# Expert stage of a Mamba-2 and mixture-of-experts layer: first weights by DMA per block, output bias in the last stage, 16 return buffers, mixed blocks in 64 columns

## The chip, the cores and the metric

The kernel runs on one core of a Trainium2 chip. The metric is the device time of one execution in microseconds. The engines are TensorE (PE, whose weight loads are shown as PEld), VectorE (DVE), ScalarE (ACT), GpSimd (POOL) and SyncE (SP), which issues most DMAs.

## The reference, cut to what matters

Input is 2048 rows of 128 values. A state-space layer with 16 heads is followed by a layer norm; its parts are not touched by the change. Then every row goes through 4 of 16 experts:

```python
logits = -dist2(x, keys) + x @ rw.T + rb            # 2048 x 16
topv, topi = top_k(logits, 4);  w = softmax(topv)
hidden = gelu(x @ w1[e].T + b1[e])                  # 128 -> 512
exp_out = hidden @ w2[e].T + b2[e]                  # 512 -> 128
fused = sum over the 4 chosen experts of w * exp_out
out = layernorm(x + fused)
```

All of it is float32. The tolerance leaves the kernel free to compute only the chosen experts.

## The kernel before, in words

The first 120 us compute the state-space layer for 16 tiles of 128 rows, in 8 pairs. For every finished tile the router finds the four experts, and POOL scatters the row, four times, with its expert numbers, row numbers and gates, to a table `xrows` in HBM that is sorted by expert (`send_one`, L1826). Two tables of blocks are built: one after five of eight pairs (`early_table`), for the first NE = 25 blocks, and one after all.

The expert stage then works on NBLK = 72 blocks of 128 rows. Blocks 0 to 63 (NF = 64) are full: all rows belong to one expert. Blocks 64 to 71 are mixed: the upper and the lower 64 rows belong to two experts. For a block b the work is

- SP reads the first row's place from the table `tbi` and issues the read of 128 rows into `xb` (`rows_in`, L446), in a ring of RB = 4
- PE turns the rows (`rows_transpose`, L741), ACT copies them from PSUM (`bt_copy`)
- DVE finds each row's gate and return address (`ids`, `row_ids`), copies the expert's first weights, their bias and the output bias, 644 columns, from the resident `w1s` into a ring (`take_w1`, L1372)
- PE multiplies by the first weights (`hidden`, L746), in four groups of 128 columns; ACT applies bias and GELU (`gelu`)
- PE multiplies by the second weights, which it reads in place from `w2s` (`expert_out`, L762)
- DVE adds the output bias (`out_bias`, L1385), ACT scales by the gate (`weigh`, L1745), POOL scatters the 128 rows to `yrows` in HBM (`give`, L1891), from one of four buffers `yw`.

Every engine runs its own list of steps, and in each step handles blocks at different lags; PE in step s turns the rows of block s+1, does the first layer of s and the second of s−1. Order inside an engine is written out by hand: steps up to 31 are single code (with parts of the router of the last two pairs of tiles between them on PE, DVE and POOL), then comes a loop of four steps per turn, then single code from step 60 on (`run_steps`, L107). Waits are on semaphores that count blocks.

The lines that the steps below touch:

```python
sp.dma_start(xb[b.slot(RB)][:], xrows[bass.ds(r, P), :]).then_inc(got[b.slot(RB)], 16)      # L465
ve.tensor_copy(w1c[r][:], w1s[:, bass.ds(expert_of(mybir.EngineType.DVE, b), 1), :]...)     # L1383
m = mm(hidden_bank(u)[:, f * P + h * HB:...], wh[:, f * P:(f + 1) * P], xbT[u][:, h * HB:(h + 1) * HB], ...)   # L755, mixed
```

Of the kernel before, what the change touches and what calls it, by code (L numbers as in the profile page):

```python
# [17 lines left out]
ALU = mybir.AluOpType  # L18
# [19 lines left out]
DE = D + 16  # L38
E, TOPK, F = 16, 4, 512
# [10 lines left out]
WB = F + FB + D  # L50
# [5 lines left out]
EPS_LN, EPS_RMS = 1e-5, 1e-6  # L56

class Step:
# [27 lines left out]

    def entry(self, h):

        return NF + 2 * (self.off - NF) + h  # L90

# [92 lines left out]
def block_and_moe(nc, d, debug=None):  # L184
    at, _ = const_table()
    with ExitStack() as ctx:
# [24 lines left out]
        w1s = sb("w1s", [D, E, WB])  # L211
# [3 lines left out]
        shared = sb("shared", [P, 8960])  # L215
# [21 lines left out]
        gmx = sb("gmx", [P, NP, 4 * HD * (CP + 1)])  # L237
        hx = sb("hx", [P, 4 * HD * (CP + 1) + CP * NP])
# [52 lines left out]
        xb = [view(ROW) for i in range(RB)]  # L291
        w1c01 = [view(WB) for i in range(2)]
        xbT = [view(P), view(P)]
        hT = [view(F), view(F)]
        sel8 = two("sel8", [P, 2, TOPK])
        idg = [sb(f"idg{i}", [P, 2]) for i in range(RB)]
        idi = [sb(f"idi{i}", [P, 1], I32) for i in range(RB)]
        yb = [view(D), view(D)]
        yw = [view(D) for i in range(RB)]
        w1c = w1c01 + [view(WB) for i in range(RB - 2)]  # L300
        w1d = [view(WB) for i in range(RB)]
        w2d = [view(FB, D) for i in range(2)]

        w1f, w2f = w1s[:].rearrange("p e f -> p (e f)"), w2s[:].rearrange("p e f d -> p (e f d)")
# [5 lines left out]
        y4 = [group_view(w1f, 0, g, TOPK * D) for g in range(NG)]  # L310
# [48 lines left out]
        def chunk_totals(g, k):  # L359
# [4 lines left out]
        ld = {k: sem("ld_" + k) for k in "cst small dtlow xT0 xT1 xT2 xT3 win wout won k idn w1 w2 b2".split()}  # L364
        zero_set, zero_out = sem("zero_set"), sem("zero_out")
# [5 lines left out]
        ksq_done, ksq_mm, kb_done, wo_done0, set_dve, ones_dve, bf_done, kw_dve, hs_set, gsum_dve, rw_dve, turn_set = (  # L371
            sem(n) for n in "ksq_done ksq_mm kb_done wo_done0 set_dve ones_dve bf_done kw_dve hs_set gsum_dve rw_dve turn_set".split())
# [6 lines left out]
        sent, sent2 = sems("sent", TOPK), sems("sent_late", TOPK)  # L379

        cnt_mm, c2, tb_mm, tab_done = (sem(n) for n in "cnt_mm c2 tb_mm tab_done".split())
        gm_set, c1, tb0_mm, var_dve, rv_pool, ge_pool = (sem(n) for n in "gm_set c1 tb0_mm var_dve rv_pool ge_pool".split())

        names3 = "bt_mm h_mm yb_mm bt_act w1_dve w2_act ht_act yb_dve yw_act c_id id_dve gt_dve"
        s3 = {n: sem(n) for n in names3.split()}
        got = sems("got", RB)
# [32 lines left out]
        def _(sp):  # L419
# [19 lines left out]

            sp.wait_ge(tab_done, 1)
            sp.wait_ge(s1["yi_mm"], NT - 2)
            for k in range(TOPK):
                sp.wait_ge(sent[k], 16 * 2 * EARLY)

# [1521 lines left out]
```

## Time and profile before

| | us |
|---|---|
| median of 3 runs (lowest, highest) | 383.8 (382.98, 385.81) |
| the profiled execution: span from first to last instruction | 313.4 |
| median less this span | 70.4 |
| PE, DVE, ACT, POOL busy | 273.5, 185.6, 214.7, 152.1 |
| mean granted clock of TensorE | 0.923 |

The profile lists the span of the profiled execution and not its own time outside it; the 70.4 us are taken from the median. The profile's page gives busy times, slices of the span, the chain of work that ended last and groups of instructions by line; the trace behind it is asked for windows, waits and single lines. "PE bank L760 x8" is eight halves issued by line 760. Register and DMA-issuing instructions of the queues are not counted as busy.

### The profile page before, as it was taken

To read this page: it belongs to the slowest core of one execution; us is meant where nothing else is said; L and a number is where in the kernel's file an instruction comes from. 1 tells how busy PE (TensorE), PEld (TensorE's weight loads), DVE (VectorE), ACT (ScalarE), POOL (GpSimd) and SP (SyncE) were. 2 spreads that over 40 slices of the span, in tenths; PEclk is the share of its full clock that TensorE was granted. 3 is DMA by queue.
4 is the path that set the end of the run, shared out by engine and by line. 5 is a ranking of instruction groups with operands and counts; after the bars stand their busy time and mean duration, and the time that the engine had idled before them with its cause. 6 is when DMAs were issued, how large, how long until landed. Compare 5 with 4: busy or idle time off the path is not lost.

```text
span 313.4 us, 11661 instructions
## 1 busy us (share of the span) xinstructions
PE 273.5 (87%) x3534; PEld 252.7 (81%) x3535; DVE 185.6 (59%) x817; ACT 214.7 (69%) x763; POOL 152.1 (49%) x167
## 2 busy tenths in 40 slices
PE   3989699988998757997996999999999999997591
PEld 3978577877787646997995999999999999995481
DVE  3135437877887865747876665566655566641272
ACT  1572538878787752784874688888888889884064
POOL 3103400037777677787677766555555564424000
PEclk9976679999999967799999799999999999999687
DMA  6999900001111212332232322222222222100973
GB/s 210 213 369 350 459 19 5 2 22 58 60 57 60 59 57 81 96 86 79 57 89 66 87 79 79 63 81 64 67 69 68 72 66 63 38 12 7 327 251 92
DMA packets 25408, 32.44 MB, mean 104 GB/s; under 512 B 4316, under 2 KB 18293, under 8 KB 25105
## 3 DMA queue, kind: packets, MB, share of 16 engines
q1 hardware_dynamic: 20576, 22.38, 24.2%
q0 software_dynamic: 4352, 8.79, 8.2%
q10 hardware_dynamic: 432, 0.67, 0.8%
q8 instruction: 26, 0.43, 0.6%
q14 instruction: 22, 0.17, 0.2%
HBM read 20.84 MB, written 11.50 MB: 103 GB/s over the span
## 4 chain that ended last, share of the span: by engine, by line
PE 74%; DVE 6%; ACT 6%; issue 6%; DMA 5%; SPq 1%; POOL 0%; ACTq 0%; POOLq 0%; DVEq 0%
PE bank L760 19%; PE bank L781 19%; PE bank L755 4%; PE bank L561 4%; PE bank L842 3%; PE bank L745 3%; ACT hs L1570 3%; PE bank L771 3%; PE bank L576 2%; PE bank L532 2%; PE bank L603 2%; PE bank L641 1%; DVE shared L962 1%; PE bank L548 1%; PE bank L845 1%
## 5 line engine op out<-in xcount | busy, mean ns | idle before, releaser
L1894 POOL DMA_INDIRECT yrows<-shared,idi x72 | 76.6, 1064 | 57.4 <-ACT shared L1752 33.3
L1826 POOL DMA_INDIRECT xrows<-rows_all,sli x64 | 62.1, 971 | 54.3 <-issue 50.7
L1733 ACT ACTIVATE shared<-bank,shared 128x128 f32<-128x128 f32 x256 | 72.9, 368 | 20.2 <-PE bank L760 19.8
L760 PE MATMUL bank<-shared 128*128 128x128 f32 x512 | 70.0, 281 | 6.0 <-issue 6.0
L760 PEld LDWEIGHTS bank<-shared 128*128 128x128 f32 x512 | 64.3, 197 | 7.3 <-issue 7.3
L781 PE MATMUL bank<-w2s,shared 128*128 x512 | 68.7, 278 | 0.1
L781 PEld LDWEIGHTS bank<-w2s,shared 128*128 128x128 f32 x512 | 63.1, 194 | 0.4 <-issue 0.3
L1383 DVE COPY shared<-w1s 128x644 f32 x64 | 33.0, 516 | 28.4 <-issue 27.3
L1752 ACT ACTIVATE shared<-shared,idg 128x128 f32<-128x128 f32 x72 | 30.0, 419 | 9.3 <-DVE shared L1396 7.9
L962 DVE TENSOR_TENSOR shared<-bank,small 128x512 f32<-128x512 f32 x32 | 21.2, 683 | 5.4 <-PE bank L576 5.2
L1719 ACT ACTIVATE shared<-bank 128x128 f32<-128x128 f32 x72 | 20.8, 289 | 4.5 <-PE bank L745 4.3
L745 PE MATMUL bank<-cst,shared 128*128 128x128 f32 x72 | 20.4, 283 | 2.0 <-DMA shared<-xrows 2.0
L561 PE MATMUL bank<-xT_all,winT 128*128 128x128 f32 x128 | 19.8, 304 | 2.0 <-issue 2.0
L561 PEld LDWEIGHTS bank<-xT_all,winT 128*128 128x128 f32 x128 | 17.6, 213 | 3.1 <-issue 3.1
L1396 DVE TENSOR_TENSOR shared<-bank,shared 128x128 f32<-128x128 f32 x64 | 18.4, 287 | 2.1 <-PE bank L781 0.5
L1364 DVE TENSOR_REDUCE idg<-sel 128x2 f32<-128x8 f32 x72 | 11.6, 161 | 11.6 <-ACT shared L1752 9.0
L1570 ACT ACTIVATE hs<-hx 32x128 f32<-32x128 f32 x32 | 13.8, 432 | 3.7 <-DVE hx L956 3.4
L1729 ACT ACTIVATE shared<-bank,shared 128x64 f32<-128x64 f32 x64 | 14.0, 330 | 2.5 <-PE bank L755 2.1
L755 PEld LDWEIGHTS bank<-shared 128*128 128x128 f32 x128 | 15.2, 194 | 0.2 <-issue 0.2
L755 PE MATMUL bank<-shared 128*128 128x64 f32 x128 | 15.3, 272 | 0.0
L1357 DVE SCALAR_TENSOR_TENSOR sel<-shared,tb 128x8 f32<-128x8 f32 x64 | 14.0, 218 | 1.9 <-issue 1.8
L576 PE MATMUL bank<-shared 32*64 32x128 f32 x512 | 12.8, 313 | 1.5 <-DVE hx L949 1.5
(233 smaller groups left out, 480.2 us busy)
## 6 DMA issues: line engine op xcount, KB each, us to landing
shared<-xrows SPq DMA_DIRECT2D x64, 70.0 KB
w1s<-in_w1T SPq DMA_DIRECT2D x1, 4128.0 KB, 23.0
w2s<-in_w2T SPq DMA_DIRECT2D x1, 4096.0 KB, 23.1
w1s<-yrows SPq DMA_DIRECT2D x8, 512.0 KB, 6.8
yrows<-shared,idi POOLq DMA_INDIRECT x72
xrows<-zrow SPq DMA_DIRECT2D x1, 1120.0 KB, 11.9
w1s<-in_b SPq DMA_DIRECT2D x1, 1024.0 KB, 22.4
xrows<-rows_all,sli POOLq DMA_INDIRECT x64, 2.4
```

Of the source, the lines that this page charges most:

```text
L561: m = mm(bank[2][:, k * P:(k + 1) * P], winT[:, c0:c0 + P], xT_all[:, t * P:(t + 1) * P], start=True, stop=True)
L745: pe.transpose(turned_rows(), xb[b.slot(RB)][:, 0:D], ident).then_inc(s3["bt_mm"], 1)
L755: m = mm(hidden_bank(u)[:, f * P + h * HB:f * P + (h + 1) * HB], wh[:, f * P:(f + 1) * P], xbT[u][:, h * HB:(h + 1) * HB], start=True, sto ...
L760: m = mm(hidden_bank(u)[:, f * P:(f + 1) * P], w[:, f * P:(f + 1) * P], xbT[u][:, :], start=True, stop=True)
L781: m = mm(out_bank(u), hT[u][:, f * P:(f + 1) * P], w2s[:, bass.ds(ex, 1), f, :], start=(f == 0), stop=(f == FB - 1))
L962: tt(sc[t % 4][:, r * HH:(r + 1) * HH, :].rearrange("p (b h) i -> p b h i", b=2), two_banks.rearrange("p b (h i) -> p b h i", h=H // 4), s ...
L1383: ve.tensor_copy(w1c[r][:], w1s[:, bass.ds(expert_of(mybir.EngineType.DVE, b), 1), :].rearrange("p o f -> p (o f)")).then_inc(s3["w1_dve"], 1)
L1570: m = act(hs[m_ % 2][rows, :, :, r * 2 * HD:(r + 1) * 2 * HD], chunk_states(m_)[rows, :, :, 0:CP].rearrange("p (j a) w c -> p c j (a w)", ...
L1733: m = act(hT[u][:, f * P:(f + 1) * P], hidden_bank(u)[:, f * P:(f + 1) * P], ACT.Gelu, bias=w[:, F + f:F + f + 1])
L1752: act(yw[r][:], yb[u][:], cp, scale=idg[r][:, 1:2]).then_inc(s3["yw_act"], 1)
L1826: po.indirect_dma_start(out=xrows, out_offset=bass.IndirectOffsetOnAxis(ap=sli[:, g, k:k + 1], axis=0), in_=rows_all[:, g, :], in_offset=N ...
L1894: po.indirect_dma_start(out=yrows, out_offset=bass.IndirectOffsetOnAxis(ap=idi[r][:, 0:1], axis=0), in_=yw[r][:, :], in_offset=None, bound ...
```

## The change

1. The first weights are no longer resident. SP issues, besides the row read, one DMA per full block from HBM (128 x 516 words, 258 KB) into a ring of four, and one for each of the 16 half blocks into 16 places that last until the end: seven in steps 25 to 31, eight in steps 56 to 63, one in step 64. PE waits for all 16 before the first mixed block.
2. The output bias leaves the blocks. DVE builds a 2048 x 16 table of gates in six operations in steps 25 to 30, PE turns it in step 31, and the last stage adds gates times b2 with eight products more. b2 lies in a block-diagonal buffer `b2d`, written by POOL's memset and eight small DMAs at the start.
3. DVE scales the block's output straight from PSUM (`weigh`); ACT's scaling and DVE's addition go.
4. The blocks before 30 return through 16 buffers, the later ones through 8.
5. In mixed blocks the first layer is cut into 64 output columns (16 products of 64 x 64 instead of 8 of 128 x 64), the rows are turned by two products, and the copy of the second expert's w2 moves from ACT to DVE.
6. POOL's root for the last tiles comes after six sends of tile pair 6 instead of eight; its eight last sends follow each other instead of alternating with returns. Some router functions on DVE change places. SP's loop is eight steps long, and the check of the table's value is left out.

```diff
-WB = F + FB + D
+WB = F + FB
...
+            def weights_in(b):
+                if b.had(RB):
+                    sp.wait_ge(s3["ht_act"], b.back(RB).count())
+                ex = expert_at(mybir.EngineType.SP, b.val())
+                sp.dma_start(w1c[b.slot(RB)], d["w1T"][:, bass.ds(ex, 1), :].rearrange("p o f -> p (o f)")
+                             ).then_inc(got_w[b.slot(RB)], 16)
...
+            def step3(s):
+                if s.live(NBLK):
+                    rows_in(s)
+                if s.back(1).live(NF):
+                    weights_in(s.back(1))
+                if s.peeled and NE <= s.off < LO3:
+                    mixed_weights_in(s.off - NE)
+                if s.peeled and NF - 8 <= s.off < NF:
+                    mixed_weights_in(LO3 - NE + s.off - NF + 8)
+                if s.peeled and s.off == NF:
+                    mixed_weights_in(2 * NM - 1)
...
-                pe.wait_ge(s3["w1_dve"], b.count())
...
+                    pe.wait_ge(ld["mixed"], 16 * 2 * NM)
                     for f in range(FB):
-                        for h, wh in enumerate((w, w1d[b.slot(RB)])):
-                            m = mm(hidden_bank(u)[:, f * P + h * HB:f * P + (h + 1) * HB], wh[:, f * P:(f + 1) * P],
-                                   xbT[u][:, h * HB:(h + 1) * HB], start=True, stop=True, skip_group_check=True)
+                        for h in range(2):
+                            for c_ in range(2):
+                                m = mm(hidden_bank(u)[c_ * HB:(c_ + 1) * HB, f * P + h * HB:f * P + (h + 1) * HB],
+                                       w1m[b.half(h)][:, f * P + c_ * HB:f * P + (c_ + 1) * HB],
+                                       xbT[u][:, h * HB:(h + 1) * HB], start=True, stop=True, skip_group_check=True)
...
+                pe.wait_ge(got_w[b.slot(RB)], b.weights_got(RB))
...
+            pe.wait_ge(gT_act, 1)
+            pe.wait_ge(ld["b2"], 16 * 8)
             for g in range(NG):
+                mm(to, gT[:, g // 4, :], b2d[:, k:k + GT * D].rearrange("p (t d) -> p t d", t=GT), start=False, stop=False)
...
+            def weigh(b):
+                ve.wait_ge(s3["yb_mm"], b.count())
+                if not b.early_ring() or b.last_put() > 0:
+                    ve.wait_ge(put[b.home()], b.last_put())
+                ts_(yw[b.home()][:], out_bank(b.slot(2)), idg[b.slot(RB)][:, 1:2], None, ALU.mult).then_inc(s3["yw_dve"], 1)
...
             def step3(s):
-                for fn, lag in ((ids, 0), (take_w1, -1), (row_ids, 2), (out_bias, 2)):
...
+                if s.back(-1).live(NBLK):
+                    ids(s.back(-1))
+                    row_ids(s.back(-1))
+                if s.back(1).live(NBLK):
+                    take_w2(s.back(1))
+                if s.back(2).live(NBLK):
+                    weigh(s.back(2))
```

On SP, one step of the loop was a table read, its check and address (ISA rows), and the row read (`shared` holds `xb`):

```order
L464 ISA
L464 TENSOR_LOAD tbi
L464 ISA x2
L465 ISA
L465 DMA shared<-xrows 128x140
```

Now the same step holds two table reads and two DMAs (`xbw` is the ring of rows, `w1r` the ring of first weights):

```order
L484 ISA
L484 TENSOR_LOAD tbi
L502 ISA
L502 DMA xbw<-xrows 128x140
L455 ISA
L455 TENSOR_LOAD tbi
L508 ISA
L508 DMA w1r<-in_w1T 128x516
```

The check of the value (`L464 ISA x2`) is gone, a table read and a DMA are added. In steps 25 to 31 and 56 to 63 a third pair follows, into the buffer `y4w` of the mixed blocks' weights:

```order
L484 TENSOR_LOAD tbi
L502 ISA
L502 DMA xbw<-xrows 128x140
L455 TENSOR_LOAD tbi
L508 ISA
L508 DMA w1r<-in_w1T 128x516
L455 TENSOR_LOAD tbi
L513 ISA
L513 DMA y4w<-in_w1T 128x516
```

On PE, a step of the mixed blocks began with the transposition of the next block's rows and the first layer in eight products:

```order
L745 MATMUL bank<-cst,shared 128x128
L755 MATMUL bank<-shared 128x64 x8
L412 TENSOR_LOAD tbi
L771 ISA
L771 MATMUL bank<-w2s,shared 64x128
L771 MATMUL bank<-shared 64x128
```

Now the rows are turned by two products, and the first layer has sixteen:

```order
L812 MATMUL bank<-cst,xbw 64x128 x2
L827 MATMUL bank<-shared,y4w 64x64 x16
L455 TENSOR_LOAD tbi
L845 ISA
L845 MATMUL bank<-w2s,shared 64x128
L845 MATMUL bank<-shared 64x128
```

The second layer (L771, now L845) is the same, and every product of the step now has 64 output columns. On DVE, a step of a full block was a copy of weights among five other operations:

```order
L1357 SCALAR_TENSOR_TENSOR sel<-shared,tb 128x8
L1364 TENSOR_REDUCE idg<-sel 128x2
L412 TENSOR_LOAD tbi
L1383 ISA
L1383 COPY shared<-w1s 128x644
L1371 TENSOR_TENSOR idi<-idg,pen 128x1
L1396 TENSOR_TENSOR shared<-bank,shared 128x128
```

Now four operations remain, and the last reads PSUM and the gate:

```order
L1445 SCALAR_TENSOR_TENSOR sel<-xbw,tb 128x8
L1451 TENSOR_REDUCE idg<-sel 128x2
L1458 TENSOR_TENSOR idi<-idg,pen 128x1
L1463 TENSOR_SCALAR shared<-bank,idg 128x128
```

The copy with its table read is gone, and gate and address of a block are computed one step before its rows are multiplied.

## Rows read from the trace of the kernel before

**Rows 1.** The page: PE's busy tenths and its granted clock in 40 slices.

```profile
PE   3989699988998757997996999999999999997591
PEclk9976679999999967799999799999999999999687
```

**Rows 2.** Five stretches: busy time of each engine, granted clock, DMA share, GB/s.

```profile
core 0: us, PE busy (x) PEld busy (x) DVE busy (x) ACT busy (x) POOL busy (x), PEclk, DMA share, GB/s
124.60:177.40 52.80, 46.62 (x401) 44.69 (x402) 36.61 (x191) 35.69 (x133) 39.32 (x40) 0.94 0.30 82
177.40:259.00 81.60, 81.60 (x734) 81.60 (x734) 49.17 (x217) 68.69 (x259) 46.41 (x44) 1.00 0.25 71
259.00:285.00 26.00, 24.93 (x273) 22.95 (x271) 14.34 (x55) 22.69 (x91) 10.23 (x10) 1.00 0.14 34
285.00:289.50 4.50, 3.69 (x16) 2.96 (x16) 0.51 (x2) 1.69 (x2) 2.65 (x3) 1.00 0.02 0
293.20:298.70 5.50, 5.50 (x13) 4.42 (x14) 1.89 (x7) 0.50 (x2) 0.00 (x0) 0.50 1.04 388
```

**Rows 3.** Chain of waits, two full steps and a mixed one: start, duration, what.

```profile
255.45 0.89 PE bank L760 x8
...
257.35 0.89 PE bank L760 x8
...
265.05 1.73 PE bank L755 x16
266.79 1.02 PE bank L771 x16
...
268.07 1.73 PE bank L755 x16
```

**Rows 4.** The page's groups: DVE's copy of weights; busy, mean ns, idle before.

```profile
L1383 DVE COPY shared<-w1s 128x644 f32 x64 | 33.0, 516 | 28.4 <-issue 27.3
```

**Rows 5.** Waits in 125 to 178 us: total, times, longest.

```profile
PEld bank L760 <- issue: 7.3, 6, 2.9
DVE rw L1023 <- POOL rv L1900: 3.2, 1, 3.2
```

**Rows 6.** Chain of waits on SP: the second row read from its table read on.

```profile
121.90 0.38 SPq L464
...
122.31 0.16 SPq L464
...
122.59 0.04 SPq L465
...
122.74 1.89 DMA shared<-xrows
```

**Rows 7.** DMA instructions on SP by line: ns least, median, most.

```profile
L465 SPq DMA_DIRECT2D shared<-xrows x64: 332/333/358, 121.5 to 249.5; - x64
L461 SPq DMA_DIRECT2D shared<-xrows x16: 477/477/566, 251.4 to 271.1; - x16
L474 SPq DMA_DIRECT2D w1s<-yrows x8: 400/472/583, 289.5 to 293.2; - x8
```

**Rows 8.** SP's own waits in 190 to 250 us: total, times, longest.

```profile
SPq L457 <- DVE idg L1364: 17.3, 31, 0.8
```

**Rows 9.** Chain: 64 x 64 products; page: GELU of mixed blocks.

```profile
52.90 0.69 PE bank L603 x16
...
L1729 ACT ACTIVATE shared<-bank,shared 128x64 f32<-128x64 f32 x64 | 14.0, 330 | 2.5 <-PE bank L755 2.1
```

**Rows 10.** Chain of waits at the end; output DMAs on SP.

```profile
283.79 1.11 PE bank L771 x16
...
287.28 2.11 DMA yrows<-shared,idi
...
289.47 3.69 DMA w1s<-yrows
...
L479 SPq DMA_DIRECT2D out<-w2s x16: 596/606/709, 300.8 to 310.9; - x16
```

More of the change, by code:

```diff
@@ L56, with early_puts @@
 EPS_LN, EPS_RMS = 1e-5, 1e-6
+def early_puts(home):
+    return len([b for b in range(EARLY_HOMES) if b % RE == home])
 class Step:
@@ L473, in _ @@
+            sp.wait_ge(tab_done, 1)
+            for k in range(TOPK):
+                sp.wait_ge(sent[k], 16 * 2 * EARLY)
+            run_steps(sp, step3, NF - 1, RY, LO3, NBLK)
+            for j in range(RE):
+                late_puts = len([b for b in range(EARLY_HOMES, NBLK) if b % RY == j])
+                sp.wait_ge(put[j], 16 * (early_puts(j) + late_puts))
             for g in range(NG):
@@ L778, in expert_out @@
                 if b.had(2):
[L779 removed]
+                    pe.wait_ge(s3["yw_dve"], b.back(2).count())
                 for f in range(FB):
@@ L1385, in out_bias @@
-            def out_bias(b):
-                u = b.slot(2)
-                ve.wait_ge(s3["yb_mm"], b.count())
-                if b.had(2):
-                    ve.wait_ge(s3["yw_act"], b.back(2).count())
-                if b.mixed():
-                    for h, wh in enumerate((w1c[b.slot(RB)], w1d[b.slot(RB)])):
-                        r = slice(h * HB, (h + 1) * HB)
-                        m = tt(yb[u][r, :], out_bank(u)[r, :], wh[r, F + FB:WB], ALU.add)
-                    m.then_inc(s3["yb_dve"], 1)
-                    return
-                tt(yb[u][:], out_bank(u), w1c[b.slot(RB)][:, F + FB:WB], ALU.add).then_inc(s3["yb_dve"], 1)
@@ new lines, in take_w2, with gate_rows @@
+            def take_w2(b):
+                if not b.mixed():
+                    return
+                if b.off >= NF + 2:
+                    ve.wait_ge(s3["yb_mm"], b.back(2).count())
+                ex = expert_at(mybir.EngineType.DVE, b.entry(1))
+                ve.tensor_copy(w2d[b.slot(2)][:].rearrange("p f d -> p (f d)"),
+                               w2s[:, bass.ds(ex, 1), :, :].rearrange("p o f d -> p (o f d)")).then_inc(s3["w2_dve"], 1)
+            def gate_rows(k):
+                h, what = divmod(k, 3)
+                t = slice(h * NT // 2, (h + 1) * NT // 2)
+                if k == 0:
+                    ve.wait_ge(s1["pk_act"], NP - 2)
+                if k > 0:
+                    ve.wait_ge(g_dve, k)
+                if what == 0:
+                    m = tt(gq, c("eids").rearrange("p (k e) -> p k e", k=TOPK).unsqueeze(1).broadcast_to([P, NT // 2, TOPK, E]),
+                           rows_all[:, t, RA:RI].unsqueeze(3).broadcast_to([P, NT // 2, TOPK, E]), ALU.is_equal)
+                if what == 1:
+                    m = tt(gq, gq, rows_all[:, t, RG:ROW].unsqueeze(3).broadcast_to([P, NT // 2, TOPK, E]), ALU.mult)
+                if what == 2:
+                    m = ve.tensor_reduce(gd16[:, h * P:(h + 1) * P].rearrange("p (t e) -> p t e", e=E),
+                                         gq.rearrange("p t k e -> p t e k"), AX_X, ALU.add)
+                m.then_inc(g_dve, 1)
```

317 lines of the change are left out of this document (166 added, 151 removed).

## The prediction

> **What bounds the kernel now.** I read the slices and the busy shares first: TensorE (PE) is busy in nine tenths of nearly every slice from the third on, and its granted clock is full except near 30, 125 and 295 us [rows 1]. Then a table by stretch [rows 2]. It cuts the expert stage in three. In 124.6 to 177.4 us, steps 0 to 20, PE is busy for 46.6 of 52.8 us. In 177.4 to 259.0, steps 21 to 63, it is busy for all 81.6 us. In 259.0 to 285.0 come the eight mixed blocks. After that PE works 3.7 us, stops, and runs at half clock until 298.7.
>
> The chain of waits shows what one step is. A full block repeats after 1.90 us (255.45 to 257.35; its first layer is eight halves in 0.89 us), a mixed one after 3.02 us, of which the first layer takes 1.73 and the second 1.02 [rows 3]. So in the middle 43 steps nothing but PE sets the time, and work taken off DVE or ACT gives nothing there. It can give something in steps 0 to 20, and the change can lose something anywhere if a new wait lasts longer than 1.90 us per block.
>
> **The change part by part.** One execution is worked through: its span is 313.4 us; the median of the runs is 383.8, so 70.4 us lie around the span and I leave them alone. Differences are made against the span.
>
> *First weights by DMA, steps 0 to 20.* DVE loses one copy per block: 0.516 us busy and, before it, 27.3/60 = 0.46 us for the register load of the expert's number [rows 4]. ACT loses the scaling of outputs. 21 steps at 1.90 are 39.8 us, the other PE work there (two groups of position counts, a transposition, an output product, the table) about 2.7, so 10.3 us of the 52.8 are surplus: PE waiting, and running at half clock (mean 0.94). What ended PE's waits at L760 is "issue", 7.3 us in 6 waits of the weight load, longest 2.9: these are waits for DVE's copy, which sat behind other DVE work, once behind the 3.2 us in which DVE waited for POOL's root of the last variance [rows 5]. POOL now computes that root two sends earlier. With about 0.9 us of DVE taken out of each step, DVE has room for the routing work between blocks. The 16 homes let POOL send its eight late rows in one go without holding DVE. I take half of the surplus as gone, 5.5 us; bounds 2 and 9. A new cost stands at the start: the first weights can be asked for only after two row reads. From 120.44 the two items and half a third end near 123.05, the transfer lands 2.4 us later (below) at 125.45, and block 0's first layer began at 125.00: +0.5. Net −5.0.
>
> *What SP has to issue, steps 21 to 64.* This is the part that speaks against the change. One row read on SP, from the table read at 121.90 to the landing transfer's issue at 122.74, is 0.84 us, plus 0.33 for the DMA instruction and 0.05 [rows 6, 7]. The usual table read is 0.27, not 0.38, and the address check (122.31 to 122.59, 0.28 us) goes. One item of the new kind is therefore 0.11 less and 0.28 less: 1.22 − 0.39 = 0.83 us. The wait for rows adds 0.05. A straight-written step is two items, 1.71 us; in the loop register arithmetic adds some 0.09 per item, and the branch 0.05 per block, so 1.96 us. Steps 25 to 31 and 56 to 63 carry a third item (a mixed block's weights): 2.55 us. Before, SP had room: in 60 us it waited 17.3 us over 31 blocks for DVE, 0.56 us a block [rows 8]. That room, plus the check, is 0.84; the added item is 0.83 and its registers 0.09. So SP is now longer than PE's 1.90.
>
> How much may SP lag? The ring of four weights is free for block b when the GELU of b−4 ends: the first layer ends 1.0 us into step b−4, ACT's whole work of a step is 68.69/43 = 1.60 us, nearly all of it GELU, so some 2.5 us into that step; 0.45 to the issue, then the transfer. Its landing I take as 1.89 us, the row read's [rows 6], plus the additional 188 KB at 388 GB/s [rows 2], 0.5: 2.4 (bounds 1.9 and the 3.7 of a 512 KB return [rows 10]). Needed at 7.7 us: slack 2.3. From the start of step 21, SP's third item of step 25 ends at 2.3 us, the next six steps at 17.6, 24 loop steps at 64.6, eight steps of three items at 85.0, step 64 (two half row reads at 0.83 + 0.14, since 64 partitions cost 0.477 against 0.333 [rows 7], and two weight items) at 88.7, the rows of block 65 at 90.7. They land 1.4 us later, so step 64 cannot start before 92.3. PE alone would need 81.5. So +10.8 us.
>
> The unknown is the instruction that issues 128 x 516 words from HBM: no row shows it. The nearest is the row read through a register, also 128 partitions, 0.333 us; returns are at 0.472 [rows 7]. I take 0.333 because form and register match. At 0.472 and some queue pressure (up to 0.583) 55 items cost up to 10 us more; at 0.30, a loop without branch cost, and a quicker landing, 4 us less, and if SP's overhead overlaps in a way I don't see, the whole 10.8 goes.
>
> What a page says here: the Trainium skill, DMA: Bandwidth & Descriptors, section Rules for kernel authors, says that spreading DMAs over several issuing engines doesn't help bandwidth and only saves the sequencer's issue time. By that rule issue time is a price of its own and one engine has to pay all of it; the trace agrees, with a landing of 1.9 us but the same 0.33 us instruction on each read. A reader who thinks of bandwidth alone (258 KB at 388 GB/s is 0.68 us of each 1.90, on top of a DMA share of 0.25) would put this part at nothing.
>
> *Mixed blocks.* Before, 16 halves with 128 weight columns and 64 moving ones take 1.73 us. After, 32 halves of 64 x 64. The same shape stands at L603: 16 halves in 0.69 us, the wait for the first result included [rows 9]. Bounds are 2 x 0.69 = 1.38 and 0.9 (twice what remains of 0.69 without about 0.24 of filling); I take 1.1. Two turned row halves replace a transposition, about equal. So a mixed step is 1.1 + 1.02 + 0.2 = 2.3 against 3.02. ACT has 14.0/8 = 1.75 us of GELU per mixed block [rows 9] and a copy of 0.29: under 2.3. DVE gets the copy of w2, but it ends about when PE wants it. SP's two half reads take 2.0. Six steps gain 0.72, step 64 0.7, the last one 0.85: −5.9.
>
> The Trainium skill, TensorEngine Tiling (Array Packing), section Restrictions, says column tiling disables the fast weight load. If 64-column loads were as long as L755's, 32 x 0.108 = 3.5 us, the mixed blocks would be 1.7 us slower each. L603 contradicts it: its 16 in 0.69 us are 0.043 each.
>
> *The end.* From the last expert product to the first read of returned rows are now 4.6 us: 284.9 to 289.47 [rows 10], with two steps on DVE, one on ACT and POOL still sending the block before. One DVE product from PSUM, 0.3, then the send and its landing 2.1, POOL free: 3.1. −1.5. The waits for 16 homes instead of 4 add up to 0.4, contained.
>
> *Last stage.* PE gets eight products of 256 columns, as long as the eight it has: 3.7 us [rows 2]. They lie before the first y4 data and beside its transfer, in a hole of 3.7 us. I also expect a gain: after that hole PE ran 5.5 us at half clock [rows 2], and the first output left late, after which SP issues sixteen outputs at 0.61 [rows 10] without a break. A filled hole keeps the clock at 2.4 GHz; half of 5.5 us comes back, less 0.6 for the last added product: −2.2. If the clock falls anyway, the added products cost up to +3.
>
> Sum: −5.0 + 10.8 − 5.9 − 1.5 − 2.2 = −3.8. Span 309.6, time 380.0 us. The earlier parts (5 MB less at the start, a longer POOL memset, six DVE products of 512 columns, two more transpositions) lie in gaps or under SP's queue and count zero; without that cover they cost 1 to 3 us.
>
> **Rivals.**
> 1. *SP keeps up.* If an item is 0.75 instead of 0.83, loop steps are 1.80 and only the three-item steps lag, mostly inside the slack of 2.3. For it: SP's instructions are short and the row queue waited 0.56 us a block. Against: the sum above is from single rows. Time 380.0 − 10.8 + 2 = 371.2.
> 2. *SP's weight issue is dear: slower.* Each of 39 block weights and 16 mixed ones takes 0.52 us (between 0.472 and 0.583) instead of 0.333. It decides from about 0.40 us, where the whole gain is used up. PE then waits over 2.1 us a step from step 21. 380.0 + 55 x 0.19 = 390.4.
> 3. *The early stage doesn't speed up*, because POOL's sends (0.97 us each, one after another) or DVE's order still set it: +5, 385.
> 4. *The change does nothing for mixed blocks*, weight loads being in line: +6 to +14 (the page's rule), 386 to 394. L603 speaks against it.
>
> **How the numbers follow.** Forecast 0.48, rival 1 0.18, rival 2 0.16, rival 3 0.14, rival 4 0.04. The forecast's own spread is 375 to 386, from item lengths of 0.80 to 0.87 over 95 items and the bounds of the early gain. A measurement of this kernel can tell about 1%, 3.8 us, from no change. Faster than 380.0: half of the forecast (0.24), all of rival 1 and a little of 3: 0.46. Slower than 387.6: rivals 2 and 4 and a little of the forecast: 0.20. The rest 0.34. The range takes in rival 1 and most of rival 2: 369 to 391.
>
> **What would show it.** PE's steps in the middle should grow from 1.90 to about 1.96 in the loop and 2.55 in steps 25 to 31 and 56 to 63, with PE waiting for w1 transfers, and SP's queue should stop waiting for DVE. Mixed steps at 2.3; the step before the first of them long. Steps 0 to 20 in 47 to 48 us. Granted clock full between 293 and 299. Wrong, if middle steps stay at 1.90 (rival 1), if SP's DMA for w1 is above 0.40 (rival 2), or if PE's surplus early stays at 10 us (rival 3).

## The result, and the profile after

The changed kernel takes 395.5 us (median of 4 runs, 394.88 to 398.84), the kernel before 383.39 (4 runs, 382.23 to 385.81): a ratio of 1.032, 95% interval 1.028 to 1.037. It is slower, and the time lies above my range of 369 to 391. Some kernels ran in two states a per cent or two apart, and the ratios here and below compare only executions in the faster one, so that they can differ a little from the quotient of the medians.

The profiled execution of the changed kernel took 395.21 us, and its span is 393.4. Only 1.8 us lie around the span. That alone overturns a sentence of the prediction, "70.4 us lie around the span": had it been so before, it would be so now. The page of the changed kernel:

```profile
span 393.4 us, 11573 instructions
PE 300.7 (76%) x3704; PEld 268.9 (68%) x3705; DVE 164.7 (42%) x742; ACT 190.3 (48%) x684; POOL 146.3 (37%) x168
PE   4987997594948583446499419998999987889893
PEclk9956899577786868585789857999999998999998
L834 PE MATMUL bank<-shared,w1r 128*128 128x128 f32 x512 | 73.7, 290 | 7.2 <-DMA w1r<-in_w1T 6.7
```

In rows 1, PE was busy in nine tenths of nearly every slice. Here it is not from the seventh slice (about 60 us) to the twenty-fourth, and the granted clock goes up and down. What runs there first is the scan of the state-space layer, which the change does not touch; the row sends begin in that slice (66.1 us). The last line is the first expert layer (L760 before): it waits 6.7 us for weights from HBM, the new wait that I had forecast.

I timed the middle and the mixed steps by when PE begins to turn the rows of a block (L816, and L812 for mixed ones). So "step 21" below is the start of that piece for block 21, and "steps 21 to 64" is the time from there to the same piece of block 64. (In the prediction a step begins when the rows of the block after it are turned, so its steps lie one block later.)

### The profile page after: what moved, and what is told of

The parts are those of the page before. It is cut to its first block, busy times and chain, and to the rows that moved or that the text cites. A ratio compares the mean times of both kernels' runs of the same rounds, so it can differ in the third digit from the quotient of the medians.

```text
span 393.4 us, 11573 instructions
## 1 busy us (share of the span) xinstructions
PE 300.7 (76%) x3704; PEld 268.9 (68%) x3705; DVE 164.7 (42%) x742; ACT 190.3 (48%) x684; POOL 146.3 (37%) x168
## 4 chain that ended last, share of the span: by engine, by line
PE 54%; issue 19%; SPq 11%; DMA 5%; ACT 4%; DVE 3%; another core or an unknown queue 2%; ACTq 0%; DVEq 0%; POOLq 0%; POOL 0%
PE bank L834 9%; PE bank L855 9%; PE bank L626 5%; PE bank L641 5%; SPq L455 3%; SPq L508 2%; PE bank L845 2%; PE bank L687 2%; SPq L502 2%; SPq L484 2%; PE bank L827 2%; PE bank L613 2%; ACT hs L1666 2%; DMA y4w<-yrows 2%
## 5 line engine op out<-in xcount | busy, mean ns | idle before, releaser
L1979 POOL DMA_INDIRECT yrows<-shared,idi x72 | 70.5, 979 | 83.2 <-DVE idi L1458 39.2
L1829 ACT ACTIVATE shared<-bank,w1r 128x128 f32<-128x128 f32 x256 | 72.9, 368 | 57.4 <-PE bank L834 34.7
L834 PE MATMUL bank<-shared,w1r 128*128 128x128 f32 x512 | 73.7, 290 | 7.2 <-DMA w1r<-in_w1T 6.7
L834 PEld LDWEIGHTS bank<-shared,w1r 128*128 128x128 f32 x512 | 66.9, 204 | 9.9 <-issue 8.1
L1463 DVE TENSOR_SCALAR shared<-bank,idg 128x128 f32<-128x128 f32 x72 | 25.2, 350 | 74.1 <-remote 24.6
L1815 ACT ACTIVATE shared<-bank 128x128 f32<-128x128 f32 x72 | 20.9, 291 | 29.6 <-remote 15.1
L816 PE MATMUL bank<-cst,xbw 128*128 128x128 f32 x64 | 18.7, 292 | 14.7 <-ACT shared L1815 7.7
L641 PEld LDWEIGHTS bank<-shared 32*64 32x64 f32 x512 | 12.9, 169 | 19.4 <-issue 18.6
L1050 DVE TENSOR_TENSOR shared<-bank,small 128x512 f32<-128x512 f32 x32 | 21.2, 683 | 10.1 <-PE bank L641 10.1
L626 PEld LDWEIGHTS bank<-xT_all,winT 128*128 128x128 f32 x128 | 21.5, 253 | 2.8 <-issue 2.6
L816 PEld LDWEIGHTS bank<-cst,xbw 128*128 128x128 f32 x64 | 9.4, 147 | 16.3 <-issue 16.2
L1445 DVE SCALAR_TENSOR_TENSOR sel<-xbw,tb 128x8 f32<-128x8 f32 x64 | 14.2, 221 | 13.2 <-DMA xbw<-xrows 10.5
L687 PE MATMUL bank<-shared,xz 128*16 128x64 f32 x512 | 13.8, 235 | 6.5 <-issue 3.8
L687 PEld LDWEIGHTS bank<-shared,xz 128*16 128x16 f32 x512 | 9.6, 104 | 8.6 <-issue 8.5
L1825 ACT ACTIVATE shared<-bank,y4w 128x64 f32<-128x64 f32 x64 | 14.0, 329 | 2.4 <-PE bank L827 2.1
```

The lines of the kernel that those rows point to most:

```text
L626: m = mm(bank[2][:, k * P:(k + 1) * P], winT[:, c0:c0 + P], xT_all[:, t * P:(t + 1) * P], start=True, stop=True)
L641: m = mm(bank[b][q * Q:(q + 1) * Q, j * P:(j + 1) * P], c_[rows, 2 + j, q * Q:(q + 1) * Q], cbd[t % 2][rows, j, q, :], start=True, stop=Tr ...
L687: m = mm(turned_y[32 * c_:32 * c_ + NC * HD, a * Q:(a + 1) * Q], xz[t % 4][:, h * NC * HD:(h + 1) * NC * HD], sc[t % 4][:, a % 2 * 8 + a / ...
L816: pe.transpose(turned_rows(), xb[b.slot(RB)][:, 0:D], ident).then_inc(s3["bt_mm"], 1)
L834: m = mm(hidden_bank(u)[:, f * P:(f + 1) * P], w[:, f * P:(f + 1) * P], xbT[u][:, :], start=True, stop=True)
L1050: tt(sc[t % 4][:, r * HH:(r + 1) * HH, :].rearrange("p (b h) i -> p b h i", b=2), two_banks.rearrange("p b (h i) -> p b h i", h=H // 4), s ...
```

## The experiments

**Is the base right? The two kernels once more.** No edit.

> The kernel before, unchanged, profiled and timed again. Theory A: every timed execution near 383 us has a span near 381 us, in which the scan stage runs slowly from the first row send (66 us) on, with pairs about 21 us apart as in the profile of the changed kernel; the span of 313.4 that I predicted from is of another, rarer kind of execution. Then the two kernels have to be compared with the slow scan in both, and the change costs 12 us against about 381. Theory B: the span is 313 in every execution and 70 us lie outside it; then the changed kernel's slow scan (pairs 21 us apart, 1.8 us outside the span) is something that the change brought in.

> The changed kernel, unchanged. Theory A: one more execution near 395 with pairs 21 us apart; there is a chance of one near 322 (395 less the 70 us), with pairs 10.6 us apart, as the kernel before showed once. Theory B: always 395.

Measured: before again 382.59 us (10 runs), its profiled span 384.0, beside 385.83 for that execution. The changed kernel 396.05, ratio 1.030 (1.021 to 1.040). Theory A holds. By stretch, the kernel before on this chip (scan from the fourth pair to step 0, early steps, middle, mixed, end; then the eight row sends of one pair, and the rest of that pair):

```profile
64.20:169.50 105.30, 67.17 (x1217) 53.63 (x1217) 44.05 (x189) 41.52 (x151) 41.52 (x43) 0.74 0.10 32
169.50:245.50 76.00, 52.15 (x388) 50.18 (x387) 37.52 (x196) 34.88 (x130) 40.08 (x40) 0.78 0.19 56
245.50:328.90 83.40, 82.14 (x734) 81.73 (x732) 48.57 (x216) 68.75 (x259) 47.78 (x44) 1.00 0.24 69
67.40:77.70 10.30, 5.82 (x92) 3.51 (x90) 0.70 (x2) 2.01 (x9) 7.90 (x8) 0.71 0.15 50
77.70:88.80 11.10, 9.53 (x162) 8.14 (x159) 7.56 (x30) 6.24 (x22) 0.00 (x0) 0.81 0.03 9
```

The columns are those of rows 2: length, then busy time and instructions of PE, PEld, DVE, ACT and POOL, the clock, the DMA share and GB/s. The same stretches in the profile that I predicted from:

```profile
63.50:123.60 60.10, 50.32 (x1217) 43.18 (x1217) 44.84 (x194) 41.96 (x151) 41.85 (x44) 0.91 0.17 56
66.70:76.80 10.10, 9.18 (x248) 7.97 (x247) 7.97 (x32) 8.17 (x29) 7.88 (x8) 1.00 0.16 54
```

The 1217 matmuls of the scan take 105.3 us here and 60.1 there. While eight row sends go, PE gets through 92 matmuls instead of 248. The weight loads of two neighbouring lines of the program show it, in the kernel before on this chip (start, length; in brackets the idle time before):

```profile
71.61 0.18 PEld L681 LDWEIGHTS bank<-oh,ones 128*128 128x128 bf16 x4 [0.51 <-issue]
71.81 0.18 PEld L576 LDWEIGHTS bank<-shared 32*64 32x64 f32 x1
72.35 0.30 PEld L576 LDWEIGHTS bank<-shared 32*64 32x64 f32 x3 [0.36 <-issue]
73.07 0.30 PEld L576 LDWEIGHTS bank<-shared 32*64 32x64 f32 x5 [0.42 <-issue]
74.52 0.34 PEld L576 LDWEIGHTS bank<-shared 32*64 32x64 f32 x5 [1.14 <-issue]
75.97 0.30 PEld L576 LDWEIGHTS bank<-shared 32*64 32x64 f32 x4 [1.10 <-issue]
```

Three to five pieces, a pause of 0.4 to 1.1 us in which PE waits for nothing that the profile shows, then the next few. The clock falls only afterwards: from 69.1 to 70.5 us it is still full, and PE gets through 9 matmuls.

```profile
69.10:70.50 1.40, 0.53 (x9) 0.37 (x9) 0.05 (x1) 0.34 (x1) 1.10 (x2) 1.00 0.29 95
```

I call this the slow supply.

**Do the row sends cause it?** POOL in `send`, before its first send (the paced waits go):

```
+                if m_ == 0:
+                    po.wait_ge(s1["yi_mm"], NT - 4)
```

> The kernel before, with POOL's 48 early row sends held back until the state products of pair 5 are done, so that none runs beside the scan of pairs 0 to 5. If PE's slow scan comes from the row sends running beside it: pairs stay 10.6 us apart through 106 us, and the sends (48 x 1.26 = 61 us, from about 106) delay the first expert block to about 170; time 383 +- 10, but the scan fast. If it has nothing to do with the sends: pairs are 21 us apart from 66 us on although POOL is idle, the first block comes near 230, time about 440.

Measured: 389.2 us (one execution). Pairs are 10.6 us apart up to 95.8, and from the first send (95.5) the next one takes 53 us. First block at 174.6. Here 32 sends follow each other without a break, up to 135.8, and the longer the row, the slower PE gets: from 106 to 126 us it does 19 matmuls, where a pair of 10.6 us has some 250. Its full pace is back at 140.6, about 5 us after the last of them:

```profile
85.20:95.80 10.60, 9.64 (x252) 8.38 (x253) 8.50 (x35) 8.70 (x31) 0.33 (x1) 1.00 0.01 3
106.00:116.00 10.00, 2.42 (x12) 0.97 (x11) 0.00 (x0) 0.00 (x0) 7.56 (x9) 0.50 0.17 58
116.00:126.00 10.00, 1.37 (x7) 0.72 (x7) 0.39 (x1) 0.00 (x0) 7.56 (x9) 0.50 0.17 59
138.00:149.00 11.00, 8.85 (x151) 7.67 (x152) 5.38 (x25) 4.01 (x12) 0.00 (x0) 0.61 0.00 1
```

So the slow supply comes with the sends and goes after them, and its cost is not a fixed one per send.

**Does the burst of the last pair's sends make the change's steps 15 to 17 long?** Only POOL's order is put back:

```
-            for b in range(3, 5):
+            for b in range(3, 7):
                 moe(b)
...
                 send_one(7, i)
+                moe(7 + i)
```

> The changed kernel with POOL's order of before for the eight row sends of the last pair: seven returns first, then a send and a return in turn. In the changed kernel's profile the eight sends stand in a row, and steps 15 to 17 take 24.4 us in place of 5.7. If the burst of sends is what stretches them: those steps come back to about 7, time 395.5 - 15 = 380. If it only delays the returns of blocks and the steps wait for DVE or for PE's own slow issue: within 3 us of 395.5.

Measured: 397.0 us, ratio 1.035 (1.028 to 1.042): no gain. From the turning of block 14 to that of block 17 (the expectation's steps 15 to 17) pass 19.9 us instead of 24.3, but 6.2 instead of 4.4 from block 9 to 11 and 2.8 instead of 1.9 from 18 to 19. The early stage comes to 76.0 us from 77.6, and the middle to 95.2 from 94.1. The delay moves with the sends.

**What do the block weights cost on SP?** In the changed kernel weights are loaded for blocks 0 to 3 only, and PE waits for a slot's first load alone; later blocks are computed with the weights that stand there, so that the output is not the layer's.

```
             def weights_in(b):
-                if b.had(RB):
-                    sp.wait_ge(s3["ht_act"], b.back(RB).count())
+                if not b.peeled or b.off >= RB:
+                    return
```

> The changed kernel, in which SP loads the first weights only for blocks 0 to 3 and later blocks use whatever stands in their ring slot (the weights of blocks 4 to 63 are left out; the mixed blocks' weights are still loaded). SP theory (an item costs SP 0.82 us, so that steps 21 to 64 last 94.1 us instead of 83.4): SP now has one item a step, one or two in 25 to 31 and 56 to 63, steps 21 to 64 come back to 82 to 84 us and the time to 395.5 - 10.5 = 385. Rival, DMA traffic (the landing is late because 258 KB per block load the queues): the same gain, so this run alone can't part them, but the landing time of the remaining transfers would fall too. Second rival, the middle steps are slowed by something other than the weights: steps 21 to 64 stay above 90 us.

Measured: 386.1 us, ratio 1.006 (1.002 to 1.010), against 1.032 with the weights (on another chip). The middle, first with the weights, then without:

```profile
248.40:342.50 94.10, 86.73 (x736) 83.89 (x733) 40.62 (x178) 57.11 (x218) 42.44 (x44) 0.98 0.78 221
```

```profile
251.70:334.60 82.90, 82.69 (x735) 82.23 (x732) 38.99 (x178) 56.68 (x218) 41.49 (x44) 1.00 0.44 120
```

94.1 and 82.9: the weights cost 11.2 us there, 9.4 in the whole. This run takes away both SP's items and the traffic (the DMA share falls from 0.78 to 0.44), so it can't part them. The timeline of SP in the changed kernel can:

```profile
255.44 0.33 SPq L502 DMA_DIRECT2D xbw<-xrows  x1
256.26 0.40 SPq L508 DMA_DIRECT2D w1r<-in_w1T  x1
257.06 0.33 SPq L513 DMA_DIRECT2D y4w<-in_w1T  x1
257.95 0.33 SPq L502 DMA_DIRECT2D xbw<-xrows  x1
258.76 0.33 SPq L508 DMA_DIRECT2D w1r<-in_w1T  x1
259.65 0.33 SPq L513 DMA_DIRECT2D y4w<-in_w1T  x1
260.52 0.33 SPq L502 DMA_DIRECT2D xbw<-xrows  x1
```

From one row read to the next 2.51 and 2.57 us, three items of about 0.83 each. (In the second group of such steps, 56 to 63, the distance is 2.5 to 2.9.) SP's waits agree, in the kernel before on the slow-supply chip and in the changed kernel:

```profile
SPq L457 <- DVE idg L1364: 14.9, 31, 0.8
```

```profile
SPq L455 <- ACT shared L1829: 0.2, 1, 0.2
```

SP no longer waits for anyone: 0.2 us in 94, and from its weight item of block 21 to that of block 63 it needs 94.8 us. So SP's own items bound the stretch. The landing adds to it in single steps: where PE idled before a first layer, in three profiles, it began 2.7 to 4.9 us after the issue of its weights. One such landing:

```profile
281.44 3.92 DMA w1r<-in_w1T
```

**Mixed blocks in 64 columns alone**, put into the kernel before (turning in two halves as well):

```
                         for h, wh in enumerate((w, w1d[b.slot(RB)])):
-                            m = mm(hidden_bank(u)[:, ...
+                            for c_ in range(2):
+                                m = mm(hidden_bank(u)[c_ * HB:(c_ + 1) * HB, ...
```

> The kernel before with only the mixed blocks' first layer and turning in 64 columns (weights still copied by DVE from SBUF). My forecast for this part alone was 2.3 us instead of 3.02 per mixed step, 5 us in all: 378. In the changed kernel's profile the mixed steps take 2.1 to 2.9, mean 2.6 without the first, and its PE waits little there, so the rival says 2.6 to 2.7 and a gain of 2.5 us: 380.5.

> The kernel before with mixed blocks in 64 columns alone, for the comparison with the changed kernel on the same chip. The mixed steps take 2.5 us instead of 3.0 on every kind of chip: 2.5 to 4 us less than before, 310.5 on a quick chip, 380.5 on a slow one.

Measured: 380.9 us, ratio 0.988 (0.983 to 0.992), and on another chip 383.0, 0.990 (0.985 to 0.995). About 1% faster, as the rival said. In the second profile the mixed steps take 2.3 to 3.1 us, mean 2.56. Their first layer (64 columns of weights, 64 moving), and PE's waits:

```profile
L762 PE MATMUL bank<-shared 128*64 128x64 f32 x192 | 7.1, 222 | 0.2 <-issue 0.2
PE bank L779 <- issue: 1.0, 3, 0.4
PE bank L762 <- issue: 0.2, 1, 0.2
```

**Half the sends.** Choices 2 and 3 are sent after all pairs:

```
+                    if i % TOPK < 2:
...
+            for m_ in range(NP - 2):
+                for i in range(2 * TOPK):
+                    if i % TOPK >= 2:
+                        send_one(m_, i)
```

> The kernel before, with half of the row sends of pairs 0 to 5 (choices 0 and 1) at their places beside the scan, and the other half (24) in a row after the last of them. Theory: PE's instructions come slowly while a row send is under way, about 1.2 us lost per send (10 us per pair of 8). Then pairs 3 to 6 are 10.6 + 5 = 15 to 16 us apart and not 21. If it is a state that one send switches on, they stay at 20 to 21. If it needs sends without a pause between them, they come to 10.6 to 12.

Measured: 392.5 us (one execution), pairs 16.8 to 17.3 us apart. With four sends beside a pair instead of eight, a pair loses 6.3 us instead of 10.1: 1.6 us per send against 1.3. It is no state that one send switches on.

**Form and size of the sends.** `ROW = D + 4 * TOPK`, and the bounds check of the returns on the row sends.

> The kernel before with rows of 144 numbers (576 bytes, a multiple of 64) instead of 140 (560 bytes) and with a bounds check on the row sends, as the returns have it, which do not slow PE in the trace. If the slow scan comes from rows of 560 bytes or from the unchecked form: pairs come back to 10.6 us apart, time near 313 to 320. If it comes from the sends as such: 21 us apart as before, time 383.

Measured: 383.4 us (one execution), pairs 20.8 to 22.1 apart. Neither this size nor this form makes the difference.

**Spacing the sends.** After each send:

```
+                po.memset(spacer[:], 0.0).then_inc(spaced, 1)
+                po.wait_ge(spaced, 2 * TOPK * m_ + i + 1)
```

> The kernel before with a small memset on POOL after each of the 64 row sends, and POOL's sequencer waiting for it before it hands on the next send, so that never two indirect DMAs stand in a row in POOL's queue. In the traces PE's slow stretches lie where indirect DMAs follow each other at 1.26 us, and none lies where returns come 1.9 us apart. Theory: it is the unbroken row that slows PE; then pairs come back to 10.6 to 12 us apart, the first expert block begins near 130 and the time is 320 to 345. Rival, each send costs PE its 1.2 us wherever it stands (half the sends cost half): pairs stay at 20 to 23, time 383 to 395.

> The kernel before with mixed blocks in 64 columns and, after every row send, a POOL memset of 640 columns that the next send waits for, so that the 64 sends start about 1.9 us apart, the distance at which the returns of blocks leave PE's steps at 1.90 us. Theory (the slow supply needs the next send within 1.3 us; at 1.9 us it stays away): the scan's pairs come back to 10.6 to 12 us, the scan ends near 125; then the 40 sends that the first block needs end at 66 + 76 + 3 = 145, the rest stand between the returns; first block 145 to 150 instead of 168, time 355 to 365. Rival (every send costs PE the same wherever it stands): pairs become longer than 21 us or stay there, the sends last longer too, time 381 to 400.

> The same kernel as e10, in which row sends start 1.9 us apart. On a quick chip: 352 again, 38 us slower than before, since POOL's sends then set the start of the expert stage. On a slow chip the question of e10 is still open: if indirect DMAs 1.9 us apart leave PE alone there, as the returns do, pairs are 10.6 to 12 us apart, the first block begins at 143 to 150 and the time is 352 to 362, 20 to 30 us under before; if every send costs PE its 1.2 us or more, 381 to 400.

The short memset (sends 1.35 us apart) gave 380.3 us beside 383.8, one run each, and pairs still 21 apart: a miss. The next run, with a longer memset (1.89 us apart), met another kind of chip. There the kernel before takes 313.9 us (7 runs, 307.99 to 315.96), and this kernel 352.7, ratio 1.141 (1.125 to 1.157): slower, its quickest run (351.7) 36 us above the slowest of the kernel before. Run again, on a chip where the kernel before takes 387.2, the same kernel takes 361.6, ratio 0.936 (0.928 to 0.945):

```profile
62.40:125.10 62.70, 52.44 (x1180) 42.82 (x1180) 42.82 (x184) 41.52 (x148) 50.85 (x63) 0.93 0.12 38
145.30:217.30 72.00, 48.58 (x386) 45.85 (x387) 36.02 (x180) 35.02 (x132) 53.16 (x61) 0.83 0.21 60
```

```profile
73.39 0.96 POOL L1836 DMA_INDIRECT xrows<-rows_all,sli  x1 [0.28 <-POOL spacer L1838]
74.36 0.65 POOL L1838 MEMSET spacer<- 128x640 f32 x1
75.28 0.96 POOL L1836 DMA_INDIRECT xrows<-rows_all,sli  x1 [0.28 <-POOL spacer L1838]
```

The scan is back to 12.5 us a pair (62.7/5; the same five pairs take 11.2 each in the profile of the quick kind), and the first block begins at 145.3 instead of 166.7.

**The changed kernel once more.**

> The changed kernel once more. The kernel before took 382 to 386 us on three chips and 314 us on a fourth, on which its scan was not slowed: the profile that I predicted from is of that kind. If this call meets such a quick chip: my steps should hold against 314 there: middle +10.7 (SP), mixed blocks -1 to -2, early stage between -5 and +1, tail and last stage -2 to -4, so 314 to 320; by my forecast alone 310. If it meets a slow chip: 395 +- 2 and pairs 21 us apart once more.

Measured: 395.7 us beside 387.2, ratio 1.027 (1.017 to 1.036), on a chip of the slow kind. On a quick chip I have not seen it.

**The change with spaced sends**, and **how close the sends may stand.**

> The changed kernel with the 64 row sends 1.9 us apart (the spacing of e12). On a slow chip: if the spacing takes PE's slow supply away here too, the first block begins near 146 as in e12. Its 16 homes let POOL hold the first returns back longer without stopping PE at step 9 (18 us there in e12), so steps 0 to 21 may take 60 to 70 instead of 72; the middle stays at 94 (SP's items), mixed steps and tail as before: 360 to 370, beside 361.6 for e12. If the change's loss of 12 us carries over whole: 372. On a quick chip about 8 us less than on a slow one.

> As e12 with a shorter memset: sends about 1.6 us apart. If the slow supply begins only below 1.6 us: pairs still 12 us apart, 0.3 us less per send over 64 sends, 361.6 - 15 = 347 on a slow chip. If 1.6 is already too close (1.35 was): pairs 18 to 21, 375 to 380.

> As e15, but the sends of pairs 6 and 7 follow each other without a memset. PE mostly waits while they go, so the row of sends costs little there: 3 to 6 us less than e15, if e15 holds; the same or slower if PE's work in steps 15 to 21 is stretched as it is in the kernel before.

Measured, with the kernel before at 384.0: 361.0 (0.939, 0.934 to 0.944), 352.3 (0.917, 0.907 to 0.927) and 348.4 (0.908, 0.902 to 0.913). At 1.64 us apart pairs are 15.2 us apart: between 1.35 and 1.89 the effect is graded. In the first of them, the change with spaced sends, PE stops 10.9 us before the rows of block 8 and 15.3 before those of block 24; POOL sends the last pair at 181 to 195 there, and sixteen returns go in a row behind it. Even so the change gains early when the sends are spaced: from block 0 to block 26 pass 84.5 us, in the mixed-block kernel with the same spacing 88.7. That is 4.2 us, near the 5.0 that I forecast; it is one profile of each. Its middle still has SP's lag (steps 26 to 64 in 82.5 us; in the mixed-block kernel with the same spacing 74.0). The last version is the fastest of all on such a chip, 35.6 us under the kernel before and 47 under the changed one. Its edit, beside that for mixed blocks, is the two lines above under `if m_ < NP - 2`, with a memset of 352 columns. On a quick chip it was not run; the 1.9 us form lost 39 us there.

## Why the prediction was wrong, point by point

*The base.* The forecast was 3.8 us less than before, measured are 12.1 more. Of the 15.9 us between them the early stage makes 7.6, the mixed blocks 3.3, the start 2, the last stage 1.5 and the end 1.3; SP's part was right. The term that failed most is "I take half of the surplus as gone, 5.5 us; bounds 2 and 9": steps 0 to 20 did not get shorter, they took 2.6 us more. Behind it stands a wrong base, "70.4 us lie around the span and I leave them alone". In every execution whose span I have seen, the time is 1.8 to 2.7 us above it. On four chips the kernel before takes 384 to 387 us in the median, on one 314; so the profile (span 313.4) was of the quick kind and the timed runs (383.8) of the other. The 70 us lie inside: 45.2 in the scan from the fourth pair on (105.3 against 60.1), 24.9 in steps 0 to 20 (76.0 against 51.1). I had the number that should have warned me, and explained it away. Whether the forecast would have held on a quick chip no run shows.

*Early stage, −5.0.* It did not come: rival 3, and of its two reasons the sends, though not by their own length but by what they do to PE. Steps 0 to 20 take 77.6, 76.5 and 80.7 us in three profiles of the changed kernel, against 76.0, 75.9 and 75.0 without the change: +2.6. DVE has less to do (31.1 us busy instead of 37.5) and it buys nothing, since PE waits while POOL sends. With spaced sends a gain of 4.2 us does show (above), which speaks for the sum over DVE's work; what it had wrong is what PE waits for on these chips. The plainest place in the changed kernel, seven returns in a row:

```profile
224.60:233.00 8.40, 1.14 (x6) 0.84 (x4) 0.10 (x1) 0.01 (x1) 6.48 (x7) 0.50 0.19 63
```

```profile
223.14 0.28 ACT L1815 ACTIVATE shared<-bank 128x128 f32<-128x128 f32 x1 [6.11 <-issue]
232.99 1.14 ACT L1829 ACTIVATE shared<-bank,w1r 128x128 f32<-128x128 f32 x4 [9.56 <-remote]
```

PE's last piece of a first layer begins at 225.3, and the GELU that needs only that starts at 232.99, with the last of seven indirect DMAs 1.28 us apart. "The 16 homes let POOL send its eight late rows in one go without holding DVE" was true, and seems harmful: the homes let returns be held back, which then go in an unbroken row. No run changes the homes alone. The returns come under the slow supply too, when they stand close. At 1.9 us apart they leave the steps at 1.90.

*SP, +10.8.* Right in kind and size. Steps 21 to 64 take 94.1, 94.1 and 94.4 us, before 83.4, 83.6 and 83.6: +10.7. The three-item step was put at 2.55 and is 2.51 to 2.57 where shown, up to 2.9 later. Loop steps, put at 1.96, come to 1.96 to 1.98 in the mean of steps 33 to 56: most stay at 1.90, a few take 2.2 to 2.7 (about steps 37 to 39). That the sum hits to 0.1 us is partly luck: the landing, taken as 2.4, was 2.7 to 4.9 where PE waited, and the kernel before takes 83.4 to 83.6 us here for what takes 82.4 in the profile that I read, by the same timing. The instruction that issues the weights, the unknown of rival 2, takes 0.336 us (mean of 64; 0.33 to 0.35 in three profiles, I took 0.333). Rivals 1 and 2 fall.

*Mixed blocks, −5.9.* Right in kind, under half in size. Alone it gave 3.2 and 4.3 us of the whole time (384.2 to 380.9, 387.2 to 383.0), of which the stage itself, from the turning of block 64 to the end of the last expert product, shows 2.3 and 2.0: 25.5 and 25.8 us instead of 27.8. Where the rest of those differences lies is open. In the change the stage takes 25.0, 25.4 and 25.1, about 2.6 less. "A mixed step is 2.3" was 2.56 alone. Its parts are as I had them: the first layer 1.1 us (330.35 to 331.45; I took 1.1), the second 1.0, the turning 0.2. Pauses of 0.2 to 0.4 us in some of the steps come on top, and I had no term for them. The profile names nothing for them there (issue, 1.0 us in 3 waits before the second layer); that PE reads the expert's number at that place is my guess at the cause. In the changed kernel SP's lag shifts the steps without adding to the stage: the turning of block 65 comes 3.3 to 3.9 us after that of 64 (before 1.9), from 64 to 71 pass 18.8, 18.9 and 18.4 us (before 19.7, alone 17.7 and 17.9), and from there to the end of the last expert product 6.3, 6.6 and 6.7 (before 8.1, alone 7.8 and 7.9). The Trainium skill, TensorEngine Tiling (Array Packing), section Restrictions, says that column tiling turns the fast weight load off; here 32 pieces of 64 columns begin within 0.90 us (351.03 to 351.93), so that price, rival 4, is not seen. The rival's own sum was too low: 1.7 us more in each of eight steps instead of a gain of 5.9 is 19.5 us above the forecast, not 6 to 14.

*The end, −1.5.* It is −0.2: from the last expert product to the first read of returned rows 4.1, 4.6 and 4.5 us, before 4.6. The last return does start 1.2 us after the product instead of 2.4. The gain is given back behind it. The last landing takes 2.5, 2.9 and 2.8 us instead of 2.1, for a cause that I did not settle. And SP goes through the waits for 16 homes in order, 0.06 us for each wait instruction; six of these stand after the one that is met last, so that 0.43 us pass from the landing to the first read instead of about 0.1 (I had the price, 0.4, and called it contained).

*Last stage, −2.2.* Not shown; −0.7 at most. From the first y4 read to the end 21.8, 22.2 and 22.2 us; before 22.7 on the same kind of chip and 23.9 in the profile that I read. But the two mixed-block kernels, whose last stage is the old one, take 22.2 and 21.5, so that 0.7 is within what single profiles scatter. The clock does stay at 2.4 GHz until 389 us or later, as forecast. But the drop that this mends, 6.9 us long in the profile that I read, is 3.5 us (365.2 to 368.7) in that of the kernel before on a chip of the slow kind: the term was worked out from a longer drop than most of these executions have.

*Start.* I put it at zero. The first block begins at 170.8, 173.0 and 166.0, before at 169.5, 167.5 and 166.7: +2 in the mean, within what single profiles scatter. Not settled.

Sum of what was measured: +2 + 2.6 + 10.7 − 2.6 − 0.2 − 0.7 = 11.8, beside a difference of 12.1; three of the six terms are no larger than the scatter of single profiles. The one loss came whole, and of 14.6 us of gains at most 3.5 came: the early one was lost under the slow supply, the others were sized too large.

## What to carry to other kernels

Compare the profiled span with the timed runs before anything else. Here the two never differed by more than 2.7 us within one execution, so that a gap of 70 us meant a profile from another kind of chip, and a sum worked out from it was not safe. Count what a DMA issue costs its sequencer (here 0.83 us with the register read) against the step it must fit in: that sum held, 10.7 us against 10.8, with some luck. And run a gain alone before trusting it in a bundle: the mixed blocks' part was worth 1%, and the bundle hid it.

## What the runs showed of the hardware

POOL's indirect DMAs, 0.96 us each and back to back, slow PE's instructions on four of the five chips that the experiments met. Pair distance in the scan, by the distance of sends, as the mean of five pairs from the fourth on: 1.89 us 12.5, 1.64 us 15.2, 1.35 us 20.9, 1.26 us 20.7. In the profile of the quick kind, with sends 1.26 us apart, these five come to 11.2 (four of 10.6 and a last one of 13.2), and without sends pairs are 10.6 apart on a slow chip too. In the kernel with sends 1.35 us apart, the first pair looks so; PE's pace comes back 1.0 us after the last send ends:

```profile
68.50:78.50 10.00, 7.43 (x56) 3.56 (x54) 0.96 (x5) 0.43 (x2) 7.47 (x14) 0.62 0.18 59
78.50:88.00 9.50, 8.63 (x151) 7.67 (x151) 7.14 (x30) 6.65 (x25) 0.22 (x1) 0.87 0.01 3
```

The slow stretch begins earlier than any data moves. In all but one of the profiles with the slow supply PE's first pause of about 0.6 us begins 0.65 to 0.71 us after the first send starts, while that send's row (1.18 us) still runs; where the sends were held back it comes later. In the kernel before, on the chip of the first experiment, it is the pause before 68.69 (the first send starts at 67.40, its first data packet at 69.15). The same place in the profile of the quick kind, where the send starts at 66.71, has no pause (second view):

```profile
67.56 0.49 PEld L622 LDWEIGHTS bank<-shared,xz 128*16 128x16 f32 x26
68.69 0.15 PEld L622 LDWEIGHTS bank<-shared,xz 128*16 128x16 f32 x6 [0.64 <-issue]
```

```profile
66.88 0.55 PEld L622 LDWEIGHTS bank<-shared,xz 128*16 128x16 f32 x32
```

The Trainium skill, Perfetto Trace Analysis, section DMA Instruction — SWDGE (GPSIMD), says that the profile's end of such an instruction is when its descriptors are written, not when the data has moved. The trace agrees: the first send's row ends at 68.58, its packets run from 69.15 to 69.50. So the slow supply is there before the first packet, and it outlasts the last one a little (in the run with 32 sends in a row by 4 us). What it takes from PE, its path to instructions or something else, no run here shows; nor why chips differ. The data packets of the sends take 0.2 us in the mean on both kinds of chip, and the 16 KB packets of the kind "instruction" 1.1 us on both, so slower transfers are not seen. It stays open, as does whether single returns 1.9 us apart would cost anything in code with more instructions per microsecond than the expert steps have.
